# A hierarchical attention layer with a scan-like feed-forward part on one core: units of the feed-forward part in another order, last gate in halves, last norm on another engine

## The chip, the cores and the metric

The kernel runs on one core of a Trainium2 chip. The metric is device time in microseconds (us) of one execution; lower is better. A core has TensorE (PE, with its weight loads PEld), VectorE (DVE), ScalarE (ACT), GpSimd (POOL) and SyncE (SP), which here issues all DMAs. Each engine works through its own queue of instructions in order, and the queues meet at semaphores.

## The reference, cut to what matters

```python
# x: 2 x 2048 tokens of 256; attention with 16 heads and hierarchical levels
x = layernorm(x + attention(x))
# feed-forward: x is read as T = 2 steps of B = 2048 rows, 256 wide
c = broadcast(in_c)
for xt in x:                                    # two steps, t = 0 and 1
    f = sigmoid(xt @ wf.T + c @ uf.T + bf)
    i = sigmoid(xt @ wi.T + c @ ui.T + bi)
    g = tanh(xt @ wc.T + c @ uc.T + bc)
    c = f * c + i * g                           # c1 after t = 0, c2 after t = 1
h = tanh(x @ wo.T + c @ uo.T + bo)              # c2's product is shared by both t
out = layernorm(x + h)
```

In the first step c is the same for every row, so `c @ u.T` is one small product (`first_bias`); in the second step it is a full one.

## The kernel before

All of x (4096 tokens) stays in SBUF as `xs`, 32 tiles of 128 tokens. Attention runs in steps s = -3 to 140 over 32 chunks; the loop over `STEPS` in each engine's program sets what it issues in a step. The feed-forward part begins at step `FIRST_FFN` = 127 and lies at first beside the last steps of attention; the order of its units is written out by hand in `ffn_units` (L114), one unit per step, all the rest in the last step. Every engine walks the same list `UNITS` and does its own share of each unit.

The 2048 rows are four blocks `blk` of 512. Products are split in three for exactness (`mm3`, L370: high x high, high x low, low x high), so each product of 256 x 256 costs, for each half `mt` of 128 output features, two k x three matmuls of 128x512.

- `("t", blk, t)`, `turn_block` (L580 PE, L807 ACT, L1137 DVE): TensorE turns four tiles of `xs` into two banks (`turned`: banks 4 and 5), ScalarE copies the high half `yH`, VectorE subtracts for the low half `yL`.
- `("g", blk, t, mt)`, `gates` (L598, L815, L1143, L1326): three gates n = 0, 1, 2 into the three banks of `ring[mt]`; for t = 1, each gate is 6 matmuls with x and then 6 with c1. `GATE` numbers these units. ScalarE applies sigmoid or tanh into `gb`; VectorE forms the new c (three operations for c2, two for c1); ScalarE copies the high half (`c1H`, `c2H`), GpSimd (VectorE in the last block) subtracts for the low half (`c1L`, `c2L`). The first c1 product of a block waits for `g_c1l`.
- `("o", n)`, `outputs` (L625, L844, L1165, L1339): 128 rows of both t. TensorE forms the c2 product (`Ba`, bank 4) and then the two x products (`Bb`, bank 5), 18 matmuls of 128x256; from n = 12 on the banks are those of `ring`. VectorE adds the bias (`cu`) and both (`hh`); ScalarE applies tanh; GpSimd adds `hh` to `xs`. One unit later `out_stats` (L1179, VectorE) and `root` (L1317, GpSimd: variance + eps, then power -0.5); two units later `out_norm` (L1190, VectorE: two `tensor_scalar`, subtract the mean and multiply), and SyncE stores the 256 KB of tiles n and n + 16 when `d_out` allows.

All elementwise helpers stand at one line per engine: L365 and L368 are TensorE's matmul and transpose, L704 ScalarE's activation, L905 and L908 VectorE's two- and three-input operations, L1257 GpSimd's two-input operation, L1193 and L1197 the two normalisations. YB (bank 5) is also attention's bank for its last projection, whose result VectorE adds into `oo`; the turn of block 1 waits for it (`d_oo`).

Of the kernel before, what the change touches and what calls it, by code (L numbers as in the profile page):

```python
# [113 lines left out]
def ffn_units():  # L114
    units = [("t", 0, 0), ("t", 0, 1), ("g", 0, 0, 0), ("g", 0, 0, 1)]
# [12 lines left out]
GATE = {u[1:]: n for n, u in enumerate([u for u in UNITS if u[0] == "g"])}  # L128
TURN = {u[1:]: n for n, u in enumerate([u for u in UNITS if u[0] == "t"])}
YUSE = {u: n for n, u in enumerate([u for u in UNITS if u[0] == "t" or (u[0] == "o" and u[1] < 16)])}  # L130


def units_at(s):
    if s < FIRST_FFN:
        return []
    if s == FIRST_FFN:
        return UNITS[:2]
    n = s - FIRST_FFN + 1
    return UNITS[n:] if s == STEPS[-1] else UNITS[n:n + 1]


def program(nc, x, xT, wqk, wtok, wout, wffn, cst, bcv, fv, out):
    ctx = ExitStack()
    with ctx:  # L144
# [34 lines left out]
        lr3 = sb("lr3", [P, NC])  # L179

# [83 lines left out]
        a_c1, a_c2, a_hh = sem("a_c1"), sem("a_c2"), sem("a_hh")  # L264
# [24 lines left out]
        def _(e):  # L289
# [73 lines left out]
        def _(e):  # L363
# [234 lines left out]
            def gates(blk, t, mt):  # L598
                y, idx = blk % 2, GATE[blk, t, mt]
                for n in range(3):  # L600
                    if idx >= 2:
                        e.wait_ge(a_g, 3 * (idx - 2) + n + 1)
                    elif n == 0:
                        e.wait_ge(d_b0, 1)
                    if n == 0:
                        e.wait_ge(d_y[1], YUSE["t", blk, t] + 1)
                    if idx == 1 and n == 1:

                        e.wait_ge(d_y[1], 2)
                    if idx == 1 and n == 2:  # L610
                        e.wait_ge(m_free[1], len([m for m, u in MISC.values() if m == 1]))
                    for k in range(2):
                        c = wcol(WF + n, mt)
                        m = mm3(ring[mt][n][:, :], wH[:, k, c], wL[:, k, c], yH[t][y][:, k, :], yL[t][y][:, k, :],
                                k == 0, k == 1 and not t)
                    if t:
                        if n == 0:
                            e.wait_ge(g_c1l, 2 * blk + 2)
                        for k in range(2):
                            c = wcol(UF + n, mt)  # L620
                            m = mm3(ring[mt][n][:, :], wH[:, k, c], wL[:, k, c], c1H[y][:, k, :], c1L[y][:, k, :],
                                    False, k == 1)
                    m.then_inc(p_gate, 1)

            def outputs(n):  # L625
# [13 lines left out]
                for k in range(2):  # L639
# [19 lines left out]
            for s in STEPS:  # L659
# [32 lines left out]
                for u in units_at(s):  # L692
                    if u[0] == "g":
                        gates(*u[1:])
# [7 lines left out]
        def _(e):  # L702
# [112 lines left out]
            def gates(blk, t, mt):  # L815
                y, idx = blk % 2, GATE[blk, t, mt]
                for n in range(3):
                    e.wait_ge(p_gate, 3 * idx + n + 1)
                    if n == 0:
                        if idx == 0:  # L820
                            e.wait_ge(d_b0, 1)
                        if blk or t:

                            p = 2 * blk + mt - (0 if t else 2)
                            if t:
# [46 lines left out]
            for s in STEPS:  # L872
# [17 lines left out]
                for u in units_at(s):  # L890
# [4 lines left out]
                    elif u[1] < 16:  # L895
                        outputs(u[1])
# [572 lines left out]
```

## Time and profile before

| | |
|---|---|
| median of 3 runs | 742.78 us (740.77 to 743.75) |
| profiled execution | 742.03 us |
| its span | 739.9 us |
| PE busy | 690.9 us (93%) |
| DVE busy | 506.7 us (68%) |
| POOL busy | 356.7 us (48%) |
| ACT busy | 323.0 us (44%) |
| first matmul of the gates | 567.69 us |
| last matmul of the outputs starts | 726.61 us |
| last vector instruction starts | 736.96 us |

The span is what the profiler recorded of one execution; the 2.1 us beside it lie before the first and after the last record. "<-" in a row stands between what an instruction writes and what it reads, or names the instruction that released it. The timelines merge like instructions (x2 and so on). The feed-forward part is what comes after about 563 us.

### The profile page before, as it was taken

To read this page: it belongs to the slowest core of one execution; us is meant where nothing else is said; L and a number is where in the kernel's file an instruction comes from. 1 tells how busy PE (TensorE), PEld (TensorE's weight loads), DVE (VectorE), ACT (ScalarE), POOL (GpSimd) and SP (SyncE) were. 2 spreads that over 40 slices of the span, in tenths; PEclk is the share of its full clock that TensorE was granted. 3 is DMA by queue.
4 is the path that set the end of the run, shared out by engine and by line. 5 is a ranking of instruction groups with operands and counts; after the bars stand their busy time and mean duration, and the time that the engine had idled before them with its cause. 6 is when DMAs were issued, how large, how long until landed. Compare 5 with 4: busy or idle time off the path is not lost. (4 is left out here: it accounts for less than half of the span.)

```text
span 739.9 us, 21966 instructions
## 1 busy us (share of the span) xinstructions
PE 690.9 (93%) x9136; PEld 597.2 (81%) x9136; DVE 506.7 (68%) x1092; ACT 323.0 (44%) x708; POOL 356.7 (48%) x462
## 2 busy tenths in 40 slices
PE   6889999999999999999999999999979899999982
PEld 3778888888888888888888888888867678787872
DVE  2754776968787777757678776969774255575757
ACT  4545444453545443454555344453533233434321
POOL 1655564645556464646546554645462234252415
PEclk9999999999999999999999999999988999999997
DMA  8123030313225030203313040311230000010102
GB/s 283 29 48 84 9 90 14 80 25 67 47 47 91 3 91 3 62 23 70 63 31 90 3 91 9 83 31 49 49 102 2 0 1 15 14 44 16 43 14 86
DMA packets 53587, 37.08 MB, mean 50 GB/s; under 512 B 5360, under 2 KB 52080, under 8 KB 53488
## 3 DMA queue, kind: packets, MB, share of 16 engines
q1 hardware_dynamic: 53488, 35.67, 19.4%
q8 instruction: 73, 1.20, 0.7%
q14 instruction: 26, 0.21, 0.1%
HBM read 30.41 MB, written 5.24 MB: 48 GB/s over the span
## 5 line engine op out<-in xcount | busy, mean ns | idle before, releaser
L365 PE MATMUL bank<-xH,wH 128*128 128x256 f32 x480 | 145.5, 303 | 1.7 <-ACT KT L704 1.5
L365 PE MATMUL bank<-xL,wH 128*128 128x256 f32 x480 | 135.3, 282 | 0.0
L365 PE MATMUL bank<-xH,wL 128*128 128x256 f32 x480 | 135.2, 282 | 0.0
L905 DVE TENSOR_TENSOR W<-bank,E 128x512 f32<-128x512 f32 x128 | 82.1, 684 | 55.6 <-PE bank L365 55.0
L365 PEld LDWEIGHTS bank<-xH,wH 128*128 128x128 f32 x480 | 90.9, 189 | 14.0 <-issue 13.2
L365 PEld LDWEIGHTS bank<-xL,wH 128*128 128x128 f32 x480 | 91.2, 190 | 0.0
L365 PEld LDWEIGHTS bank<-xH,wL 128*128 128x128 f32 x480 | 90.9, 189 | 0.0
L704 ACT ACTIVATE QT<-bank 128x512 f32<-128x512 f32 x64 | 38.2, 597 | 106.0 <-PE bank L365 106.0
L365 PE MATMUL bank<-QT,KT 64*128 64x128 f32 x1024 | 74.4, 285 | 0.0
L704 ACT ACTIVATE E<-bank 128x512 f32<-128x512 f32 x128 | 66.1, 604 | 16.6 <-PE bank L387 16.6
L704 ACT ACTIVATE KT<-bank 128x512 f32<-128x512 f32 x64 | 38.3, 598 | 79.8 <-PE bank L365 79.7
L365 PEld LDWEIGHTS bank<-QT,KT 64*128 64x128 f32 x1024 | 62.1, 187 | 11.4 <-issue 5.1
L1257 POOL TENSOR_TENSOR lr<-mv,cs 128x1 f32<-128x1 f32 (+1 forms) x80 | 17.6, 220 | 92.2 <-DVE mv L1058 75.6
L905 DVE TENSOR_TENSOR g<-g 128x512 f32<-128x512 f32 x24 | 16.6, 692 | 63.3 <-ACT g L704 63.0
L1257 POOL TENSOR_TENSOR rs<-lr,cs 128x1 f32<-128x1 f32 (+1 forms) x80 | 56.2, 703 | 6.3
L1257 POOL TENSOR_TENSOR t<-t 128x416 f32<-128x416 f32 x45 | 48.6, 1081 | 3.6
L1257 POOL TENSOR_TENSOR xL<-xt,xH 128x512 fp32r<-128x512 f32 x15 | 19.3, 1289 | 63.8 <-ACT xH L704 63.8
L419 PE MATMUL bank<-W,V 128*32 128x128 f32 x1024 | 41.7, 281 | 2.9 <-DVE oo L905 2.9
L1257 POOL TENSOR_TENSOR x<-oo,xs 128x256 f32<-128x256 f32 x32 | 23.5, 735 | 40.2 <-DVE oo L908 40.2
L1257 POOL TENSOR_TENSOR prod<-ll,cs 128x512 f32<-128x512 f32 x32 | 41.3, 1291 | 0.5 <-DVE ll L905 0.5
L905 DVE TENSOR_TENSOR pre<-bank,bv 128x208 f32<-128x208 f32 x32 | 12.0, 374 | 42.8 <-PE bank L365 42.8
L704 ACT ACTIVATE t<-t 128x416 f32<-128x416 f32 x64 | 35.1, 549 | 10.6 <-DVE t L1088 6.7
(146 smaller groups left out, 1708.6 us busy)
## 6 DMA issues: line engine op xcount, KB each, us to landing
cB<-scr SPq DMA_DIRECT2D x240, 64.0 KB, 2.9
xt<-in_xT SPq DMA_DIRECT2D x16, 256.0 KB, 3.2
xs<-in_x SPq DMA_DIRECT2D x16, 256.0 KB, 4.1
out<-xs SPq DMA_DIRECT2D x16, 256.0 KB, 2.1
xt<-in_wffn SPq DMA_DIRECT2D x8, 256.0 KB, 2.9
QT<-in_wqk SPq DMA_DIRECT2D x4, 256.0 KB, 5.9
KT<-in_wqk SPq DMA_DIRECT2D x4, 256.0 KB, 6.3
scr<-cT SPq DMA_DIRECT2D x16, 64.0 KB, 1.9
```

Of the source, the lines that this page charges most:

```text
L365: return e.matmul(o, a, b, start=start, stop=stop)
L419: y = e.matmul(YB[32 * n:32 * n + 32, 128 * k:128 * k + 128], V[sg % 3][:, c, v:v + 32], W[:, h, :], start=u == 0 and k == 0, stop=u == 1, ...
L704: return e.activation(o, i, f, **kw)
L905: return e.tensor_tensor(o, a, b, op)
L1257: return e.tensor_tensor(o, a, b, op)
```

## The change

- The unit `g` is taken apart: `x` is one gate's products with x, `c` one gate's products with c1. A list of groups (`GROUPS`) takes the place of one unit per step. For t = 1 and mt = 0 the three x products come first and then the c products; for mt = 1 x and c alternate gate by gate. Turns of t = 1 stand between two gates of a unit.
- Output units are spread: each has gates between it and the next one. An output's x products now come ahead of its c2 product.
- The last gate unit (block 3, t = 1, mt = 1) is two units `h` of 256 rows each; gates, cells, copies and subtractions are done by halves. The last four outputs use other banks (`LAST`).
- The last layernorm: GpSimd forms mean x rstd (`nm3`) after the root; ScalarE negates it (`nb3`) and normalises with scale and bias; tile 31 alone stays with VectorE (`last_norm`). In outputs 13 and 15 VectorE adds `hh` to `xs` in place of GpSimd. The stores wait for `a_out`.

The diff, cut to its core:

```diff
+def ffn_groups():
+    def g0(blk, mt):
+        return [("x", blk, 0, mt, n) for n in range(3)]
+    def g1(blk):
+        return [u for n in range(3) for u in (("x", blk, 1, 1, n), ("c", blk, 1, n))]
+    out = [[("t", 0, 0), ("t", 0, 1)], g0(0, 0), g0(0, 1)]
     for blk in range(4):
-        def o(k):
-            return ("o", 4 * blk - 4 + k) if 4 * blk - 4 + k >= 0 and blk + k // 4 > 0 else None
+        x, c = [[(k, blk) + ((1,) if k == "x" else ()) + (0, n) for n in range(3)] for k in "xc"]
+        if blk == 0:
+            out += [x, c]
+        else:
+            out += [x[0:2] + [("o", 4 * blk - 2)] + x[2:3] + c[0:1] + [("o", 4 * blk - 1)] + c[1:3]]
         if blk < 3:
-            units += [u for u in (("g", blk, 1, 0), o(3), ("t", blk + 1, 0), ("g", blk, 1, 1),
-                                  ("t", blk + 1, 1), ("g", blk + 1, 0, 0), o(4), ("g", blk + 1, 0, 1), o(5), o(6)) if u]
-        else:
-            units += [("g", blk, 1, 0), ("g", blk, 1, 1), o(3)]
-    return units + [("o", n) for n in range(12, 18)]
-UNITS = ffn_units()
-GATE = {u[1:]: n for n, u in enumerate([u for u in UNITS if u[0] == "g"])}
+            g, a = g1(blk), g0(blk + 1, 1)
+            out += [[("t", blk + 1, 0)], g[0:4] + [("t", blk + 1, 1)] + g[4:6], g0(blk + 1, 0)]
+            out += [[("o", 4 * blk)] + a[0:2] + [("o", 4 * blk + 1)] + a[2:3]]
+    return out + [[("h", h, n) for h in range(2) for n in range(3)], [("o", n) for n in range(12, 18)]]
+GROUPS = ffn_groups()
+UNITS = [u for g in GROUPS for u in g]
 TURN = {u[1:]: n for n, u in enumerate([u for u in UNITS if u[0] == "t"])}
 YUSE = {u: n for n, u in enumerate([u for u in UNITS if u[0] == "t" or (u[0] == "o" and u[1] < 16)])}
+LAST = {12: (3, 6), 13: (4, 5), 14: (7, 0), 15: (1, 2)}
...
-                e.wait_ge(d_out, n + 1)
+                e.wait_ge(a_out, n + 1)
+                if n == 15:
+                    e.wait_ge(d_out, 1)
...
+            def gate_x(blk, t, mt, n):
+                y, idx = blk % 2, 4 * blk + 2 * t + mt
+                if idx >= 2:
+                    e.wait_ge(a_g, 3 * (idx - 2) + n + 1)
+                elif n == 0:
+                    e.wait_ge(d_b0, 1)
+                if n == 0:
+                    e.wait_ge(d_y[1], YUSE["t", blk, t] + 1)
+                if idx == 1 and n == 1:
+                    e.wait_ge(d_y[1], 2)
+                if idx == 1 and n == 2:
+                    e.wait_ge(m_free[1], len([m for m, u in MISC.values() if m == 1]))
+                for k in range(2):
+                    c = wcol(WF + n, mt)
+                    m = mm3(ring[mt][n][:, :], wH[:, k, c], wL[:, k, c], yH[t][y][:, k, :], yL[t][y][:, k, :],
+                            k == 0, k == 1 and not t)
+                if not t:
                     m.then_inc(p_gate, 1)
...
+            def gate_c(blk, mt, n):
+                y = blk % 2
+                if n == 0 and mt == 0:
+                    e.wait_ge(g_c1l, 2 * blk + 2)
+                for k in range(2):
+                    c = wcol(UF + n, mt)
+                    m = mm3(ring[mt][n][:, :], wH[:, k, c], wL[:, k, c], c1H[y][:, k, :], c1L[y][:, k, :],
+                            False, k == 1)
+                m.then_inc(p_gate, 1)
...
+            def gate_h(h, n):
+                r = slice(256 * h, 256 * h + 256)
+                e.wait_ge(a_g, 3 * (13 + h) + n + 1)
+                for k in range(2):
+                    c = wcol(WF + n, 1)
+                    mm3(ring[1 - h][n][:, 0:256], wH[:, k, c], wL[:, k, c], yH[1][1][:, k, r], yL[1][1][:, k, r],
+                        k == 0, False)
+                for k in range(2):
+                    c = wcol(UF + n, 1)
+                    m = mm3(ring[1 - h][n][:, 0:256], wH[:, k, c], wL[:, k, c], c1H[1][:, k, r], c1L[1][:, k, r],
+                            False, k == 1)
+                m.then_inc(p_gate, 1)
...
             def outputs(n):
                 blk, q = n // 4, n % 4
                 y, use = blk % 2, YUSE["o", n]
                 c = slice(128 * q, 128 * q + 128)
-                Ba, Bb = banks[4:6] if n < 12 else ring[n % 2][0:2]
-                if n < 12:
-                    e.wait_ge(d_y[0], use)
+                Ba, Bb = [banks[i] for i in LAST.get(n, (4, 5))]
+                if n in (12, 14, 15):
+                    e.wait_ge(a_g, 48 if n == 12 else 51)
                 else:
-                    e.wait_ge(a_g, 3 * len(GATE))
-                    e.wait_ge(d_y[1], use - 1)
-                if blk < 3:
-                    e.wait_ge(g_c2l, 2 * blk + 2)
-                else:
-                    e.wait_ge(d_c2l, 2)
-                for k in range(2):
-                    m = mm3(Ba[:, 0:256], c2H[y][:, k, c], c2L[y][:, k, c], wH[:, k, wcol(UO)], wL[:, k, wcol(UO)],
-                            k == 0, k == 1)
-                m.then_inc(p_o, 1)
-                if n < 12:
-                    e.wait_ge(d_y[1], use)
+                    e.wait_ge(d_y[1], use if n < 12 else use - 1)
                 for t in range(2):
                     for k in range(2):
                         m = mm3(Bb[:, 256 * t:256 * t + 256], yH[t][y][:, k, c], yL[t][y][:, k, c],
                                 wH[:, k, wcol(WO)], wL[:, k, wcol(WO)], k == 0, k == 1)
+                m.then_inc(p_o, 1)
+                if blk < 3:
+                    e.wait_ge(g_c2l, 2 * blk + 2)
+                else:
+                    e.wait_ge(d_c2l, 2 if n < 14 else 3)
+                for k in range(2):
+                    m = mm3(Ba[:, 0:256], c2H[y][:, k, c], c2L[y][:, k, c], wH[:, k, wcol(UO)], wL[:, k, wcol(UO)],
+                            k == 0, k == 1)
                 m.then_inc(p_o, 1)
...
+            def gate_h(h, n):
+                r = slice(256 * h, 256 * h + 256)
+                e.wait_ge(p_gate, 45 + 3 * h + n + 1)
+                if h == 0 and n == 0:
+                    e.wait_ge(d_c1, 8)
+                act(gb[1][n][:, r], ring[1 - h][n][:, 0:256], ACT.Tanh if n == 2 else ACT.Sigmoid,
+                    bias=fvs[:, 3 + n:4 + n]).then_inc(a_g, 1)
+                if n == 2:
+                    e.wait_ge(d_c2, 8 + h)
+                    act(c2H[1][:, 1, r], gb[1][1][:, r], ACT.Copy).then_inc(a_c2, 1)
             def outputs(n):
                 i = n % 2
                 e.wait_ge(d_y[1], YUSE["o", n] + 1)
                 act(hh[i][:, :], hh[i][:, :], ACT.Tanh).then_inc(a_hh, 1)
+            def out_norm(n):
+                e.wait_ge(g_rs3, n + 1)
+                act(nb3[:, n:n + 17:16], nm3[:, n:n + 17:16], ACT.Copy, scale=-1.0).then_inc(a_nb, 1)
+                e.wait_ge(a_nb, n + 1)
+                for c in (n, n + 16) if n < 15 else (n,):
+                    a = act(xs[:, c, :], xs[:, c, :], ACT.Identity, scale=rs3[:, c:c + 1], bias=nb3[:, c:c + 1])
+                a.then_inc(a_out, 1)
...
+            def cells_h(h):
+                nonlocal made
+                f, i, c = [g[:, 256 * h:256 * h + 256] for g in gb[1]]
+                r = slice(256 * h, 256 * h + 256)
+                e.wait_ge(a_g, 45 + 3 * h + 3)
+                tt(i, i, c, ALU.mult).then_inc(d_own, 1)
+                tt(f, f, c1[1][:, 1, r], ALU.mult).then_inc(d_own, 1)
+                made += 2
+                e.wait_ge(d_own, made)
+                tt(i, f, i, ALU.add).then_inc(d_c2, 1)
+                e.wait_ge(a_c2, 8 + h)
+                tt(c2L[1][:, 1, r], i, c2H[1][:, 1, r], ALU.subtract).then_inc(d_c2l, 1)
...
             def outputs(n):
                 i, use = n % 2, YUSE["o", n]
-                Ba, Bb = banks[4:6] if n < 12 else ring[n % 2][0:2]
-                e.wait_ge(p_o, 2 * n + 1)
+                Ba, Bb = [banks[i] for i in LAST.get(n, (4, 5))]
+                e.wait_ge(p_o, 2 * n + 2)
                 if n >= 2:
                     e.wait_ge(d_y[1], YUSE["o", n - 2] + 1)
                 tt(cu[i][:, :], Ba[:, 0:256], bv[:, B_BO:B_BO + 256], ALU.add).then_inc(d_y[0], 1)
                 h3 = hh[i][:, :].rearrange("p (t n) -> p t n", t=2)
-                e.wait_ge(p_o, 2 * n + 2)
                 e.wait_ge(d_y[0], use + 1)
-                if n >= 2:
+                if n >= 2 and n - 2 != 13:
                     e.wait_ge(g_hh, n - 1)
                 tt(h3, Bb[:, :].rearrange("p (t n) -> p t n", t=2), bc(cu[i][:, :], 1, 2), ALU.add).then_inc(d_y[1], 1)
             def out_stats(n):
                 nonlocal made
                 i = n % 2
-                e.wait_ge(g_hh, n + 1)
+                if n not in (13, 15):
+                    e.wait_ge(g_hh, min(n + 1, 14))
+                else:
+                    e.wait_ge(a_hh, n + 1)
+                    dst = xs[:, n:n + 17:16, :]
+                    tt(dst, dst, hh[i][:, :].rearrange("p (t n) -> p t n", t=2), ALU.add).then_inc(d_own, 1)
+                    made += 1
+                    e.wait_ge(d_own, made)
                 for t in range(2):
                     e.bn_stats(st3[:, 2 * i + t, :], xs[:, n + 16 * t, :]).then_inc(d_own, 1)
                     made += 1
...
                 for t in range(2):
                     e.bn_aggr(mv3[:, n + 16 * t, :], st3[:, 2 * i + t, :]).then_inc(d_mv3, 1)
-            def out_norm(n):
-                nonlocal made
-                e.wait_ge(g_rs3, n + 1)
-                e.tensor_scalar(xs[:, n, :], xs[:, n, :], mv3[:, n, 0:1], rs3[:, n:n + 1], ALU.subtract,
-                                ALU.mult).then_inc(d_own, 1)
-                made += 1
-                n += 16
-                e.tensor_scalar(xs[:, n, :], xs[:, n, :], mv3[:, n, 0:1], rs3[:, n:n + 1], ALU.subtract,
+            def last_norm():
+                e.wait_ge(g_rs3, 16)
+                e.tensor_scalar(xs[:, 31, :], xs[:, 31, :], mv3[:, 31, 0:1], rs3[:, 31:32], ALU.subtract,
                                 ALU.mult).then_inc(d_out, 1)
...
-                            root(rs3[:, n:n + 17:16], lr3[:, n:n + 17:16], mv3[:, n:n + 17:16, 1], g_rs3)
+                            r = slice(n, n + 17, 16)
+                            root(rs3[:, r], lr3[:, r], mv3[:, r, 1], g_own)
+                            made += 1
+                            e.wait_ge(g_own, made)
+                            tt(nm3[:, r], mv3[:, r, 0], rs3[:, r], ALU.mult).then_inc(g_rs3, 1)
```

## Rows read from the trace of the kernel before

**Rows 1.** Busy time by stretch: PE, PEld, DVE, ACT, POOL, PE clock, DMA.

```profile
620.00:660.00 40.00, 38.26 (x207) 32.07 (x206) 24.43 (x50) 15.39 (x26) 14.66 (x18) 1.00 0.08 27
```

**Rows 2.** Waits of TensorE, 562 to 740 us: total, times, longest.

```profile
PE bank L365 <- POOL c1L L1257: 2.9, 1, 2.9
PE bank L368 <- DVE cu L905: 2.3, 2, 1.2
...
PE bank L368 <- DVE oo L905: 2.0, 1, 2.0
PE bank L365 <- DVE cu L905: 1.6, 3, 0.5
```

**Rows 3.** Timeline of TensorE: start, us, what, idle time before it and releaser.

```profile
581.41 0.50 PE L365 MATMUL bank<-c1H,wH 128*128 128x512 f32 x1 [2.89 <-POOL c1L L1257]
...
582.91 0.61 PE L365 MATMUL bank<-yH,wH 128*128 128x512 f32 x1
...
586.31 0.41 PE L365 MATMUL bank<-c1H,wL 128*128 128x512 f32 x1
...
616.67 0.39 PE L365 MATMUL bank<-wH,c2H 128*128 128x256 f32 x1 [0.52 <-DVE cu L905]
...
630.79 1.34 PE L368 MATMUL bank<-cs,xs 128*128 128x128 f32 x8 [1.16 <-DVE cu L905]
```

**Rows 4.** Busy time in a stretch of 2 us, columns as in rows 1.

```profile
584.00:586.00 2.00, 2.00 (x6) 1.51 (x6) 0.00 (x0) 0.00 (x0) 0.00 (x0) 0.50 0.00 0
```

**Rows 5.** Timeline of TensorE, end of the last gate and output 11.

```profile
711.28 0.40 PE L365 MATMUL bank<-c1L,wH 128*128 128x512 f32 x1
711.51 0.40 PE L365 MATMUL bank<-c1H,wL 128*128 128x512 f32 x1
...
713.61 0.28 PE L365 MATMUL bank<-wL,yH 128*128 128x256 f32 x1
713.73 0.28 PE L365 MATMUL bank<-wH,yL 128*128 128x256 f32 x1
```

**Rows 6.** Timeline of VectorE in the tail: one period, and the last row.

```profile
715.99 0.42 DVE L905 TENSOR_TENSOR cu<-bank,bv 128x256 f32<-128x256 f32 x1
716.50 0.69 DVE L905 TENSOR_TENSOR hh<-bank,cu 128x512 f32<-128x512 f32 x1
717.11 0.74 DVE L1184 BATCH_NORM_STATS2 st<-xs 128x6 f32<-128x256 f32 x2
...
718.05 1.31 DVE L1193 TENSOR_SCALAR xs<-xs,mv,rs 128x256 f32<-128x256 f32 x1
...
719.61 0.41 DVE L905 TENSOR_TENSOR cu<-bank,bv 128x256 f32<-128x256 f32 x1
...
736.96 0.41 DVE L1197 TENSOR_SCALAR xs<-xs,mv,rs 128x256 f32<-128x256 f32 x1
```

**Rows 7.** Timeline of GpSimd: one root among attention's end, and one period.

```profile
609.50 1.07 POOL L1257 TENSOR_TENSOR rs<-lr,cs 128x1 f32<-128x1 f32 x1
...
717.93 1.28 POOL L1257 TENSOR_TENSOR xs<-xs,hh 128x512 f32<-128x512 f32 x1 [17.72 <-ACT hh L704]
719.17 0.24 POOL L1257 TENSOR_TENSOR lr<-mv,cs 128x2 f32<-128x2 f32 x1
719.49 0.75 POOL L1257 TENSOR_TENSOR rs<-lr,cs 128x2 f32<-128x2 f32 x1
```

**Rows 8.** Groups of ScalarE: count, busy us, mean ns, idle before.

```profile
L704 ACT ACTIVATE g<-bank,fvs 128x512 f32<-128x512 f32 x24 | 16.5, 687 | 45.7 <-PE bank L365 45.4
...
L704 ACT ACTIVATE V<-bank 128x128 f32<-128x128 f32 x64 | 14.3, 275 | 33.6 <-DVE pre L905 33.6
L704 ACT ACTIVATE hh<-hh 128x512 f32<-128x512 f32 x16 | 10.1, 632 | 26.1 <-DVE hh L905 26.1
...
L704 ACT ACTIVATE yH<-bank 128x512 fp32r<-128x512 f32 x16 | 8.9, 588 | 9.4 <-PE bank L368 9.4
...
L704 ACT ACT_TABLE_LOAD x1 | 1.3, 1283 | 0.0
```

More of the change, by code:

```diff
@@ L179, in program @@
         lr3 = sb("lr3", [P, NC])
+        nm3 = sb("nm3", [P, NC])
+        nb3 = sb("nb3", [P, NC])
         first = ExitStack()
@@ L596, in turn_block @@
                     y.then_inc(p_turn, 1)
[L598 to L611, printed above, removed]
-                    for k in range(2):
[L613 to L622, printed above, removed]
-                    m.then_inc(p_gate, 1)
@@ L692, in _ @@
                 for u in units_at(s):
-                    if u[0] == "g":
-                        gates(*u[1:])
+                    if u[0] == "x":
+                        gate_x(*u[1:])
+                    elif u[0] == "c":
+                        gate_c(*u[1:])
+                    elif u[0] == "h":
+                        gate_h(*u[1:])
                     elif u[0] == "t":
@@ L813, in turn_block, with gate @@
                     act(yH[t][i][:, k, :], turned(blk, k)[:, :], ACT.Copy).then_inc(a_yh, 1)
[L815 to L825, printed above, removed]
-                                e.wait_ge(d_c1, 2 * blk + mt + 1)
-                            else:
-                                e.wait_ge(d_c2, p + 1)
-                                e.wait_ge(a_c2, p + 1)
-                                e.wait_ge(g_c2l, p + 1)
-                    bias = fvs[:, 3 * mt + n:3 * mt + n + 1] if t else b0[:, mt, n:n + 1]
-                    act(gb[mt][n][:, :], ring[mt][n][:, :], ACT.Tanh if n == 2 else ACT.Sigmoid, bias=bias).then_inc(a_g, 1)
+            def gate(blk, t, mt, n):
+                y, idx = blk % 2, 4 * blk + 2 * t + mt
+                e.wait_ge(p_gate, 3 * idx + n + 1)
+                if n == 0:
+                    if idx == 0:
+                        e.wait_ge(d_b0, 1)
+                    if blk or t:
+                        p = 2 * blk + mt - (0 if t else 2)
+                        if t:
+                            e.wait_ge(d_c1, 2 * blk + mt + 1)
+                        else:
+                            e.wait_ge(d_c2, p + 1)
+                            e.wait_ge(a_c2, p + 1)
+                            e.wait_ge(g_c2l, p + 1)
+                bias = fvs[:, 3 * mt + n:3 * mt + n + 1] if t else b0[:, mt, n:n + 1]
+                act(gb[mt][n][:, :], ring[mt][n][:, :], ACT.Tanh if n == 2 else ACT.Sigmoid, bias=bias).then_inc(a_g, 1)
+                if n < 2:
+                    return
                 if t == 0:
@@ L890, in _ @@
                 for u in units_at(s):
-                    if u[0] == "g":
-                        gates(*u[1:])
+                    if u[0] == "x" and u[2] == 0:
+                        gate(*u[1:])
+                    elif u[0] == "c":
+                        gate(u[1], 1, *u[2:])
+                    elif u[0] == "h":
+                        gate_h(*u[1:])
                     elif u[0] == "t":
                         turn_block(*u[1:])
-                    elif u[1] < 16:
-                        outputs(u[1])
+                    elif u[0] == "o":
+                        if u[1] < 16:
+                            outputs(u[1])
+                        if 0 <= u[1] - 2 < 16:
+                            out_norm(u[1] - 2)
         @block.vector
@@ L1226, in _ @@
                 for u in units_at(s):
-                    if u[0] == "g":
-                        gates(*u[1:])
+                    if u[0] == "x" and u[2] == 0 and u[4] == 2:
+                        cells(*u[1:4])
+                    elif u[0] == "c" and u[3] == 2:
+                        cells(u[1], 1, u[2])
+                    elif u[0] == "h" and u[2] == 2:
+                        cells_h(u[1])
                     elif u[0] == "t":
                         turn_block(*u[1:])
-                    else:
+                    elif u[0] == "o":
                         if u[1] < 16:
@@ L1362, in _ @@
                 for u in units_at(s):
-                    if u[0] == "g":
-                        gates(*u[1:])
+                    if u[0] == "x" and u[2] == 0 and u[4] == 2:
+                        gates(*u[1:4])
+                    elif u[0] == "c" and u[3] == 2:
+                        gates(u[1], 1, u[2])
                     elif u[0] == "o":
-                        if u[1] < 16:
+                        if u[1] < 16 and u[1] not in (13, 15):
                             outputs(u[1])
```

26 lines of the change are left out of this document (10 added, 16 removed).

## The prediction

> **What bounds the kernel now.** I read the busy table by stretches first [rows 1]: TensorE works 38.3 of 40 us in the feed-forward part, ScalarE 15.4. So that part is bound by TensorE until its matmuls end, and a tail by something else. Next come the waits of TensorE after 562 us [rows 2]: 2.9 us for `c1L` (GpSimd's low half of c1), 2.0 for `oo` (the vector add that frees bank 5 of attention's last projection), 2.3 and 1.6 for `cu` (the vector add behind which banks 4 and 5 come free). The timeline shows where they stand [rows 3]: 2.89 us before the first c1 product, then in each block 0.52 us between two output units and 1.16 us before a turn; three of the first and two of the second, 3.88 us in all, which are the 2.3 and 1.6 of [rows 2]. The 2.89 are followed by a stretch whose granted clock is 0.50, the lower level of 1.2 GHz [rows 4].
>
> The last gate's matmuls end at 711.51 + 0.23 = 711.74 us [rows 5], and the last vector instruction at 736.96 + 0.41 = 737.37 [rows 6]. The tail belongs to VectorE. Its period in [rows 6], from the `cu` at 715.99 to the next: cu 0.51, hh 0.61, two statistics and two aggregates 0.94, then both normalisations 1.56 until 719.61: 3.6 us, and 1.31 of it is the first normalisation. That first normalisation is the telling row: the same shape takes 0.41 in the last row. It starts 0.12 us after GpSimd's add of 1.28 us [rows 7] and ends 0.15 us after that add's end. The Trainium skill, SBUF — State Buffer, on the shared port pair, says that a VectorE operation in a two-port mode and a GpSimd operation block each other for a whole instruction; by that rule, the trace agrees, and the cost goes away when the normalisation leaves VectorE.
>
> The profiled execution took 742.03 us for a span of 739.9, so 2.13 lie around the span; the median of the runs is 742.78, 0.75 above it. I sum against 742.03 and add 0.75 at the end.
>
> **x products ahead of c1's.** No matmul is added. Ahead of the first c1 product, TensorE now has the x products of all three gates instead of one: 2 x 6 matmuls at 0.233 us [rows 5], 2.8 us of cover. The stall was 2.89, and attention's last projection (four matmuls) now also falls ahead of the c1 products: stall gone, -2.9. The stretch at half clock after it [rows 4] held eight matmuls from 582.91 to 586.31 us [rows 3], 3.4 us where 8 x 0.233 = 1.9: without the idle time before it, -1.5. I take both, since the stretch starts right behind the stall; that the clock dips all the same is in the range.
>
> **Turns and projection.** The projection of the last chunk stood right ahead of the turn that needs its bank, which cost the 2.0 us of `oo` [rows 2]. Now 18 matmuls (4.2 us) lie between, far more than an add of 0.42: -2.0.
>
> **Outputs apart.** In the steady blocks, between two users of banks 4 and 5 there is now gate work of at least 2.8 us. cu and hh want 0.51 + 0.69 = 1.2 us [rows 6]. The five stalls [rows 3] go: -3.9. What is late next? (a) ScalarE, in order: after an output's tanh (0.63) it now runs the sign copy and two normalisations, then the two waiting gates. Priced below, that puts the gates' end at 4.5 us after the output's matmuls, cells (0.69 x 3) at 6.6, the c2 copy at 7.2, the turned block's copies and subtractions at 9.1. TensorE wants that bank for the next turn at 9.4 (gates 2.8, a turn of about 1.0, where [rows 3] has 1.34 behind a stall, gates 5.6): 0.3 us to spare. (b) In the group o, x, x, o, x, counted from the first output's end, the second's hh is there at 6.1 us, tanh 6.7, norms 8.1, the last x gate 8.8, cells 10.2, copy 10.8, GpSimd's subtraction (1.3, as its add in [rows 7]) 12.1; TensorE wants it at 12.6 (six gate parts of 1.4 us, two outputs of 2.1): 0.5 to spare. So I take no stall, but the cover is thin.
>
> **Last gate in halves of rows.** Twelve matmuls of 512 columns become 24 of 256, 0.233 against 0.117 us [rows 5]: nothing on TensorE. The first half's cells end while the second half's matmuls run. Before, `cu` followed T0 (end of the last gate) by 715.99 - 711.74 = 4.25 us. Four VectorE steps shrink by 0.28 (0.69 to 0.41, [rows 6]), two on ScalarE by 0.2 each (512 columns 0.59, 128 columns 0.28 [rows 8], so about 0.38 for 256): 2.6 us. TensorE doesn't wait, for outputs 12 and 13 and the x part of 14 cover 5.6 us.
>
> **Output 11** moves ahead of T0: 18 matmuls at 0.117, +2.1.
>
> So T0 = 711.74 + 2.1 - 2.9 - 1.5 - 2.0 - 3.9 = 703.5.
>
> **The last norm on ScalarE, the sign and one product.** No row shows this activation with a scale and a bias from memory. A gate with a bias pointer takes 0.69, the plain copy of the same bank 0.59 [rows 8], so a pointer is 0.10. For 256 columns: 0.38 + 0.04 (from SBUF, 0.63 against 0.59) + 0.20 = 0.61, the second about 0.5 behind the first. Bounds: 0.38 without price for pointers, 0.69, a whole gate. The sign copy is between 0.2 and 0.28 [rows 8] (its 128-column row); I take 0.25 with its own wait. So 1.4 us per output on ScalarE, 2.0 with the tanh. In a sentence of its own: by the Trainium skill, ScalarE: Activation LUTs, "What ACT_TABLE_LOAD costs", an activation is 186 ns + 0.833 ns per column + 93 per pointer, which would be 0.585; the sum hardly moves. On GpSimd a product of two columns is added per output, 0.25 as `lr` [rows 7]: root and product 1.35. In outputs 13 and 15 VectorE does the add (0.69) in place of GpSimd (1.28).
>
> **The tail, from T0**, each engine in order. VectorE: cu, hh of 12 at 2.6 to 3.7, statistics 11 to 4.7, hh 13 to 5.8, statistics 12 to 6.7, hh 14 to 7.9, add and statistics 13 to 9.5, hh 15 to 10.6, statistics 14 to 11.5. ScalarE: norm 11 waits for GpSimd's root 11 (7.2), so tanh 14 ends at 9.2, norm 12 at 10.6, tanh 15 at 11.2. VectorE: add and statistics 15 to 13.1. GpSimd: add 14 to 10.5, root 13 to 11.9, root 14 to 13.2, root 15 to 14.6. Last norm on ScalarE: sign, wait, 0.61: 15.5. VectorE's last norm, 0.41, ends before it. Behind a two-input vector operation a one-column root took 1.07 us, where even a two-column one takes 0.75 [rows 7]; the adds 13 and 15 can do that once each: +0.3. The tail is 15.8 us. Before, from the same point (713.8, behind output 11) it was 737.37 - 713.8 = 23.5.
>
> The last instruction ends at 703.5 + 15.8 = 719.3; before, 2.5 us of output transfer followed; span 721.8, execution 723.9, on the median's level 724.7. I say **725**.
>
> **Rivals.** (1) The cover is thin, chance 0.25. ScalarE waits in order for GpSimd's root and for VectorE's hh; each is behind others. If (a) and (b) come 0.7 us too late in each of three blocks (+4) and the tail loses the port twice more (+2), the time is about 731. For it: GpSimd and VectorE hold each other up already [rows 6, 7]. Against: ScalarE is busy 15 of 40 us [rows 1], and the norms add 1.1 x 4 per block. (2) The clock dips as before, 0.10: +1.5, 726.5. (3) Slower, 0.04: a table switch. ScalarE loads a table for 1.28 us [rows 8]. If this activation were not in the set of sigmoid and tanh, each output would cost two loads, 2.6 us. Then (a) comes 2.3 and (b) 2.1 us too late, 13 us in three blocks, and the tail goes at 4.6 us an output on ScalarE, +9; 725 + 22 = 747. It decides as soon as a load stands between tanh and norm. Against: the copies between sigmoids needed no load, one load stands in the whole feed-forward part. By the Trainium skill, ScalarE: Activation LUTs, on table sets, identity is in every set; no row here shows this function, and it would leave 725. (4) Only one side pays, 0.05: if new waits take back all of TensorE's 10.3 us, 742.8 - 23.5 + 15.8 = 735; if the tail keeps its 23.5, 733. The forecast itself has 0.56.
>
> **Range.** Low end: the norm at 0.38 and no port loss, 721. High end: it takes in rival 1 whole, 731. Outside are rivals 3 and 4 and a part of each end. A measurement of this kernel can tell about 0.5%, 3.7 us. All cases but 3 and a worse form of 4 are over that: faster 0.92, same 0.04, slower 0.04.
>
> **What would show it.** No wait of TensorE over 0.5 us between 578 us and the tail, above all none before the first c1 product; the granted clock whole from about 567 us on to the last outputs; the last gate's end near 703.5; no normalisation of 1.3 us on VectorE; ScalarE's norm about 0.6 and no second table load; 15 to 16 us from the last gate to the last norm. Waits of ScalarE's sign copy for GpSimd ahead of gates that TensorE then waits for would make it rival 1; table loads, rival 3.

## The result, and the profile after

The changed kernel takes 720.09 us (median of 4 runs, 717.82 to 721.02) where the kernel before takes 743.26 beside it: ratio 0.9685, 95% interval 0.9654 to 0.9716, faster. I had said 725, range 721 to 731. The direction and the mechanisms held; the gain is 23 us where my sum had 18, and the time lies 0.9 us below the range. The same code ran twice more beside other experiments, at 720.33 and at 723.52 us. The page of the profiled execution (721.02 us):

```profile
span 719.2 us, 22059 instructions
...
PE 683.2 (95%) x9172; PEld 595.7 (83%) x9172; DVE 486.0 (68%) x1067; ACT 340.2 (47%) x759; POOL 356.6 (50%) x476
...
PEclk9999999999999999999999999999999899999998
```

TensorE's waits after 562 us (total, times, longest) are one row, which was there before too, at the very start of the part. All four waits of [rows 2] are gone, and so is one of 2.2 us for `c2L` in the tail of before:

```profile
PE bank L381 <- DVE yL L964: 0.7, 1, 0.7
```

Where [rows 3] had 2.89 us of idle time ahead of the first c1 product, TensorE now goes from x products to attention's last projection and on (timeline: start, us, what):

```profile
581.49 1.02 PE L378 MATMUL bank<-wo,yt 128*128 128x256 f32 x4
582.16 0.58 PE L378 MATMUL bank<-c1H,wH 128*128 128x512 f32 x1
```

The last gate ends at 701.15 us. VectorE's tail, as in [rows 6]: cu, hh and statistics follow each other in 2.0 us for the first output (2.2 for the next, 2.7 where VectorE also adds), no normalisation between them, and one at the very end.

```profile
703.89 0.42 DVE L964 TENSOR_TENSOR cu<-bank,bv 128x256 f32<-128x256 f32 x1
704.34 0.69 DVE L964 TENSOR_TENSOR hh<-bank,cu 128x512 f32<-128x512 f32 x1
704.95 0.74 DVE L1262 BATCH_NORM_STATS2 st<-xs 128x6 f32<-128x256 f32 x2
...
705.90 0.39 DVE L964 TENSOR_TENSOR cu<-bank,bv 128x256 f32<-128x256 f32 x1
...
714.22 0.25 DVE L1266 BATCH_NORM_AGGREGATE mv<-st 128x2 f32<-128x6 f32 x2
715.81 0.41 DVE L1270 TENSOR_SCALAR xs<-xs,mv,rs 128x256 f32<-128x256 f32 x1 [1.34 <-POOL nm L1334]
```

ScalarE's norm, in the tail (705.61, 705.83) and for output 15: the sign copy 0.19 to 0.21 us, one normalisation 0.60, two 1.09.

```profile
705.61 0.19 ACT L736 ACTIVATE nb<-nm 128x2 f32<-128x2 f32 x1
705.83 1.09 ACT L736 ACTIVATE xs<-xs,nb,rs 128x256 f32<-128x256 f32 x2
...
715.81 0.21 ACT L736 ACTIVATE nb<-nm 128x2 f32<-128x2 f32 x1
716.05 0.60 ACT L736 ACTIVATE xs<-xs,nb,rs 128x256 f32<-128x256 f32 x1
```

Three stretches tell more than the total. The head is all before the first gate's first matmul, which the change doesn't touch. The gate stretch goes from there to the end of the last gate. The tail goes on to the end of the last normalisation; the last store adds 2.5 us in both kernels.

| kernel | median, us | ratio to before, 95% interval | head | gate stretch | tail |
|---|---|---|---|---|---|
| before | 743.26 | 1 | 567.69 | 144.05 | 25.63 |
| changed | 720.09 | 0.9685 (0.9654 to 0.9716) | 568.01 | 133.14 | 15.50 |
| e1_together | 727.32 | 0.9811 (0.9755 to 0.9867) | 564.78 | 141.86 | 15.50 |
| e2_xfirst | 737.88 | 0.9968 (0.9932 to 1.0004) | 567.03 | 140.36 | 25.59 |
| e3_norm_act | 736.86 | 0.9932 (0.9906 to 0.9959) | 566.22 | 144.38 | 21.01 |
| e4_norm_dve | 723.60 | 0.9760 (0.9696 to 0.9824) | 564.61 | 133.14 | 18.77 |
| e5_whole | 724.64 | 0.9762 (0.9713 to 0.9811) | 567.60 | 133.01 | 21.04 |
| e6_pool_adds | 721.52 | 0.9728 (0.9655 to 0.9800) | 564.55 | 133.14 | 16.54 |
| e8_forced | 737.41 | 0.9925 (0.9895 to 0.9955) | 565.50 | 151.04 | 15.51 |
| e9_again | 723.52 | 0.9730 (0.9666 to 0.9793) | 571.70 | 133.14 | 15.51 |
| e12_control | 720.33 | 0.9696 (0.9651 to 0.9741) | 565.02 | 133.14 | 15.51 |
| e10_bias24 | 716.62 | 0.9655 (0.9616 to 0.9694) | 563.29 | 133.13 | 15.53 |
| e11_bias_split | 721.45 | 0.9696 (0.9657 to 0.9734) | 563.80 | 133.14 | 15.52 |

The medians and ratios come from the timed runs, the three stretches from one profile each. Each ratio is taken to the kernel before as it ran beside that kernel, at 743.26 us for the changed kernel, 740.88 for e1 to e4, 742.30 for e5 to e9 and 742.21 for e10 to e12, so ratios can be compared between groups and medians can't. The changed kernel ran three times (e9_again and e12_control are the same code): gate stretch and tail agree to 0.01 us, while the head moves by 6.7 us. So the stretches are what the experiments are read by.

### The profile page after: what moved, and what is told of

The parts are those of the page before. It is cut to its first block, busy times and chain, and to the rows that moved or that the text cites. A ratio compares the mean times of both kernels' runs of the same rounds, so it can differ in the third digit from the quotient of the medians.

```text
span 719.2 us, 22059 instructions
## 1 busy us (share of the span) xinstructions
PE 683.2 (95%) x9172; PEld 595.7 (83%) x9172; DVE 486.0 (68%) x1067; ACT 340.2 (47%) x759; POOL 356.6 (50%) x476
## 4 chain that ended last, share of the span: by engine, by line
PE 83%; DVE 10%; issue 3%; ACT 2%; POOL 2%; DMA 1%; SPq 0%; DVEq 0%
PE bank L378 61%; PE bank L381 6%; PE bank L400 4%; PE bank L467 4%; PE bank L432 4%; PE bank L496 3%; DVE W L964 2%; DVE S L964 1%; DVE zt L964 1%; DVE t L967 1%; DMA bv<-in_bcv 1%; ACT t L736 0%; POOL t L1334 0%; ACT E L736 0%; DVE C L1184 0%
## 5 line engine op out<-in xcount | busy, mean ns | idle before, releaser
L964 DVE TENSOR_TENSOR g<-g 128x512 f32<-128x512 f32 (+1 forms) x26 | 17.6, 676 | 35.0 <-ACT g L736 34.7
L400 PE MATMUL bank<-CT,AT 32*128 32x128 f32 x1024 | 38.5, 288 | 2.0 <-DVE CT L1189 2.0
```

The lines of the kernel that those rows point to most:

```text
L400: m = e.matmul(XP[q][:, :].rearrange("p (h t) -> p h t", h=H)[:, :, 8 * j:8 * j + 8], AT[b][r, j, :], CT[b][r, :].rearrange("p (h t) -> p ...
L964: return e.tensor_tensor(o, a, b, op)
```

## The experiments

The prediction's sum for the gate stretch was 144.05 + 2.1 - 2.9 - 1.5 - 2.0 - 3.9 = 135.85 us. Measured: 133.14. So 2.7 us of the 4.6 that I missed lie there (the tail and the time around the span give 0.3 each, the head takes 0.3 back, and the rest is the step to the median). Theory R, the prediction's: a stall costs what its idle row says. Theory S: it costs more, from the last matmul's start to the time at which the flow is regular again. The rival: the outputs' stalls have no part in it. The rows of the kernel before already speak for S, when starts are compared instead of idle times (TensorE, first between two outputs, then at a turn):

```profile
615.87 0.28 PE L365 MATMUL bank<-wH,yL 128*128 128x256 f32 x1
616.67 0.39 PE L365 MATMUL bank<-wH,c2H 128*128 128x256 f32 x1 [0.52 <-DVE cu L905]
616.89 0.28 PE L365 MATMUL bank<-wL,c2H 128*128 128x256 f32 x1
...
630.79 1.34 PE L368 MATMUL bank<-cs,xs 128*128 128x128 f32 x8 [1.16 <-DVE cu L905]
631.89 0.48 PE L365 MATMUL bank<-yH,wH 128*128 128x512 f32 x1
```

The row of 615.87 is a matmul of 256 columns, regularly followed by the next after 0.117 us. It was followed after 0.80: 0.68 lost, and the row says 0.52, since a matmul's record (0.28 us) is longer than the spacing. The first matmul after the stall takes 0.22 to the next start instead of 0.117: 0.10 more. At the turn the eight transposes and what follows them take 1.10 us where an unstalled turn takes 0.79: 0.31 more.

**One kind of stall, eleven times.**

```diff
                 m.then_inc(p_o, 1)
+                if n < 11:
+                    e.wait_ge(d_y[1], use + 1)
```

> The changed kernel with a wait added to TensorE: behind each of outputs 0 to 10 it waits until VectorE has written that output's hh, so eleven stalls of one known kind stand in the steady blocks. Theory R (a stall costs its idle row): the stretch from the first gate to the end of the last one grows by the sum of the idle rows, about 11 x 1.2 = 13 us. Theory S (a stall costs from start to start): it grows by about 0.3 us more for each, 16 to 17 us. If the clock falls behind idle times of this length, it grows by more than that; the kernel before had none behind its stalls of 1.2 us.

The idle rows sum to 14.4 us (waits of TensorE):

```profile
PE bank L378 <- DVE hh L966: 14.4, 11, 1.5
```

The gate stretch grew by 17.9 us. In this run it began at half clock, which cost its first three matmuls 0.6 (0.60, 0.43 and 0.38 us from start to start instead of 0.34, 0.23 and 0.23). The other 17.3 are 2.9 more than the idle rows, 0.26 us for each stall. One of them, from start to start:

```profile
607.61 0.28 PE L378 MATMUL bank<-wH,c2L 128*128 128x256 f32 x1
609.13 0.50 PE L378 MATMUL bank<-yH,wH 128*128 128x512 f32 x1 [1.24 <-DVE hh L966]
609.47 0.40 PE L378 MATMUL bank<-yL,wH 128*128 128x512 f32 x1
```

1.52 us where 0.117 is regular, then 0.34 where 0.233 is: 1.51 lost for a row of 1.24. Theory S holds. The granted clock stayed whole behind all eleven.

**The outputs back together.**

```diff
-            out += [x[0:2] + [("o", 4 * blk - 2)] + x[2:3] + c[0:1] + [("o", 4 * blk - 1)] + c[1:3]]
+            out += [[("o", 4 * blk - 2)] + x + c + [("o", 4 * blk - 1)]]
...
-            out += [[("o", 4 * blk)] + a[0:2] + [("o", 4 * blk + 1)] + a[2:3]]
+            out += [[("o", 4 * blk)] + a + [("o", 4 * blk + 1)]]
```

> The changed kernel with the output units put back next to each other, as they stood before (outputs 1 and 2, 5 and 6, 9 and 10 in pairs; 3 and 7 right before a turn); all else as changed. Theory R (a stall costs its idle row, as the prediction summed it): five stalls, 3.9 us, so the last gate ends about 705.0 us and the time is 724. Theory S (a stall costs from start to start, with the refill behind it and the slower first matmuls): 0.87 x 3 + 1.71 x 2 = 6.0 us, time 726. Theory N (the two us that the prediction missed have nothing to do with the outputs' place): 3.9 or less, and the excess over the nominal spacing stays below 0.2 us beside the idle rows.

```profile
PE bank L378 <- DVE hh L964: 4.0, 3, 1.4
PE bank L381 <- DVE cu L964: 2.3, 2, 1.2
```

The stretch grew by 8.7 us, 0.8 of them again a start at half clock. So 7.9 for idle rows of 6.3: 1.6 more for five stalls, 0.32 each. The rows themselves are not those of before: with its x products first, an output waits in bank 5 for the previous output's hh (1.25 to 1.4 us), where before it waited in bank 4 for cu (0.52). So both sizes that I had expected, 3.9 and 6.0, were too low, but their order stands: the cost exceeds the rows. The place of the outputs sets it.

**The x products first, alone.** In the kernel before, TensorE's loop over the three gates of a unit (t = 1, mt = 0) forms all x products and only then the c1 products.

```diff
...
+                    if t and mt == 0 and n < 2:
+                        continue
+                    for n in range(3) if t and mt == 0 else [n] if t else []:
...
```

> The kernel before with one change: for t = 1 and mt = 0 TensorE issues the x products of all three gates ahead of the first c1 product. If the clock's dip follows from the idle time ahead of it, stall and dip go together: 3.1 + 1.6 = -4.7 us, 738.5. If the dip comes anyway: -3.1, 740. If the wait only moves (c1L comes as late and the 2.8 us do not cover it, or the turn's stall grows): above 741.

The gate stretch is 3.7 us shorter, 4.3 without the 0.6 that its start at half clock cost (first row: busy times, then the granted clock). Where [rows 4] has 0.50, the clock is now whole:

```profile
566.00:568.00 2.00, 2.00 (x19) 1.42 (x19) 1.60 (x3) 1.86 (x2) 0.00 (x0) 0.50 0.03 8
...
582.00:584.00 2.00, 2.00 (x10) 1.64 (x9) 0.00 (x0) 0.69 (x1) 0.12 (x1) 1.00 0.00 0
584.00:586.00 2.00, 2.00 (x10) 1.61 (x10) 0.00 (x0) 0.79 (x2) 0.00 (x0) 1.00 0.00 0
```

The dip followed the idle time: stall and dip went together. The 4.3 compare with 2.9 + 1.5 in the sum. They are not all that the stall and the dip cost: without the projection ahead of it, the first c1 product still came 0.52 us behind the last x product where 0.233 is regular (580.88 to 581.40 us), and its first gap was 0.10 longer. With these the two cost 4.7, as Theory S has it (3.2 + 1.5). The ratio's interval includes 1, so the median proves nothing here; the reading rests on the stretch of one profile.

**The norm on ScalarE, alone.** The kernel before with the changed kernel's sign copy, normalisations and product.

```diff
+            def out_norm(n):
+                e.wait_ge(g_rs3, n + 1)
+                act(nb3[:, n:n + 17:16], nm3[:, n:n + 17:16], ACT.Copy, scale=-1.0).then_inc(a_nb, 1)
...
```

> The kernel before with one change: the last norm of all 16 outputs on ScalarE (sign copy, scale and bias), the product on GpSimd. Stalls of TensorE stay. Tail: VectorE's period falls from 3.6 to 2.1 us, and GpSimd becomes the bound at 1.3 + 1.35 = 2.65 us per output: 5 x 1.0 = -5 us, 738. If the norm's removal gives the whole 1.5 us per output: -7.5, 735.5. If ScalarE's waits for GpSimd hold up the gates in the steady blocks: above 740.

The tail fell by 4.6 us and the gate stretch grew by 0.3. GpSimd is the bound, as expected: it works without a pause at 2.4 us per output, and VectorE waits for its add (1.38 us, last row).

```profile
726.57 1.26 POOL L1268 TENSOR_TENSOR xs<-xs,hh 128x512 f32<-128x512 f32 x1
727.79 0.19 POOL L1268 TENSOR_TENSOR lr<-mv,cs 128x2 f32<-128x2 f32 x1
728.06 0.70 POOL L1268 TENSOR_TENSOR rs<-lr,cs 128x2 f32<-128x2 f32 x1
728.83 0.20 POOL L1268 TENSOR_TENSOR nm<-mv,rs 128x2 f32<-128x2 f32 x1
```

```profile
727.86 0.75 DVE L1197 BATCH_NORM_STATS2 st<-xs 128x6 f32<-128x256 f32 x2 [1.38 <-POOL xs L1268]
```

**The norm back on VectorE.**

```diff
-                        if u[1] == 17:
-                            last_norm()
+                        if 0 <= u[1] - 2 < 16:
+                            out_norm(u[1] - 2)
...
```

> The changed kernel with the last norm back on VectorE (two operations per output, no sign copy, no product on GpSimd); outputs apart, halves and x first stay. Tail: five norms of 1.56 us come back on VectorE, less what GpSimd bound: +5 to +7 us, 725 to 727. In the steady blocks nothing if the new places cover VectorE's 1.56 us more per output; stalls before the turns otherwise, +1 per block.

Gate stretch the same to 0.01 us: the new places of the outputs cover VectorE's norms as well. Tail +3.3 us, less than the 5 to 7. The reason stands in VectorE's rows: of the first norms of six outputs only the one that starts right behind the start of GpSimd's add takes 1.32 us. One more, at 709.40 us, meets the last 0.4 us of an add and takes 0.57. The others take 0.38 to 0.41, since with the adds of 13 and 15 on VectorE there are fewer to meet.

```profile
702.50 1.32 DVE L1267 TENSOR_SCALAR xs<-xs,mv,rs 128x256 f32<-128x256 f32 x1
...
706.06 0.38 DVE L1267 TENSOR_SCALAR xs<-xs,mv,rs 128x256 f32<-128x256 f32 x1
...
712.21 0.38 DVE L1267 TENSOR_SCALAR xs<-xs,mv,rs 128x256 f32<-128x256 f32 x1
```

By the rule of the Trainium skill on the shared port pair (SBUF — State Buffer, "Who interferes with whom"), the trace agrees: the same operation costs 0.38 or 1.32 us by what GpSimd does at that moment.

**The last gate whole.** One unit of 512 rows; output 12 starts in banks that are free.

```diff
-    return out + [[("h", h, n) for h in range(2) for n in range(3)], [("o", n) for n in range(12, 18)]]
+    return out + [g1(3), [("o", n) for n in range(12, 18)]]
...
-LAST = {12: (3, 6), 13: (4, 5), 14: (7, 0), 15: (1, 2)}
+LAST = {12: (0, 1), 13: (4, 5), 14: (2, 3), 15: (6, 7)}
...
```

> The changed kernel with the last gate unit whole (512 rows, as before) and the banks of the last four outputs chosen so that output 12 can start at once; all else as changed. The prediction's term: the first cu comes 4.25 us behind the last gate where the halves give 2.75: +1.5 us in the tail, by VectorE. Rival: TensorE stalls for c2L behind output 12's x part (about 3 us idle), its clock falls, outputs 13 to 15 come late and the tail grows by 3 us or more.

The tail grew by 5.5 us, so the rival won. TensorE waits for c2L and its granted clock falls to 0.50; VectorE, which no longer has the norms to do, waits for TensorE twice:

```profile
705.00 0.58 PE L378 MATMUL bank<-wH,c2H 128*128 128x256 f32 x1 [2.81 <-DVE c2L L964]
```

```profile
706.00:708.00 2.00, 2.00 (x12) 2.00 (x11) 1.28 (x3) 0.13 (x1) 0.00 (x0) 0.50 0.00 0
```

```profile
706.68 0.42 DVE L964 TENSOR_TENSOR cu<-bank,bv 128x256 f32<-128x256 f32 x1 [1.74 <-PE bank L378]
...
710.52 0.42 DVE L964 TENSOR_TENSOR cu<-bank,bv 128x256 f32<-128x256 f32 x1 [1.75 <-PE bank L378]
```

How much of the 5.5 us is the stall and how much the clock, this run doesn't separate. The kernel before had such a stall too, with the clock at 0.51 from 716 to 718 us behind it:

```profile
PE bank L365 <- DVE c2L L905: 2.2, 1, 2.2
```

There VectorE needed 3.6 us per output, and none of its rows in the tail has a wait for TensorE of over 0.1 us. My term for the halves, 4.25 to 2.6 us, was the part on VectorE. The sum stood all the same, because I had worked out the new tail as a whole.

**The adds of 13 and 15 on GpSimd.**

```diff
-                        if u[1] < 16 and u[1] not in (13, 15):
+                        if u[1] < 16:
...
```

> The changed kernel with the adds of outputs 13 and 15 back on GpSimd. GpSimd's add takes 1.28 us where VectorE's takes 0.68, and output 15's add is on the last chain: +0.6 to +1 us in the tail if the chain through VectorE is bound by its work, 0 to +0.3 if VectorE's freed 1.3 us makes up for it, and more than +1.5 if GpSimd (root and product of 12 to 14) is busy when the add could start.

Tail +1.03 us, the upper end of the first case. VectorE now waits for GpSimd's add before each of the last three statistics (0.38 us for the first of them):

```profile
708.54 0.75 DVE L1255 BATCH_NORM_STATS2 st<-xs 128x6 f32<-128x256 f32 x2 [0.35 <-POOL xs L1327]
...
710.97 0.75 DVE L1255 BATCH_NORM_STATS2 st<-xs 128x6 f32<-128x256 f32 x2 [1.39 <-POOL xs L1327]
```

**The same code again, and the head.**

> The changed kernel once more, beside the three above. From the first gate to the end: 151.2 us as in its first profile, within 0.3. The place of the first gate (568.0 us then, 567.7 before, 564.6 to 567 in the other runs) lies ahead of everything that was changed: if it moves by 2 us or more between runs of the same kernel, the part of the miss that is not in the feed-forward part is that.

> The changed kernel without any edit, on the same chip as the two above. From its first gate to the end 151.2 us, as in both profiles of it; in the place of the first gate anything between 564 and 572 us.

Gate stretch plus tail plus store: 151.20 and 151.18 us, as in the first profile. The first gate stood at 571.70 and at 565.02. In e9_again the granted clock was at half from about 556 to 569.5 us:

```profile
558.00:562.00 4.00, 4.00 (x21) 4.00 (x20) 1.88 (x5) 0.00 (x0) 3.20 (x4) 0.50 0.00 0
...
566.00:570.00 4.00, 3.35 (x14) 2.60 (x13) 1.98 (x6) 1.19 (x2) 0.74 (x2) 0.56 0.00 0
```

In there lie the 36 matmuls of two columns of `first_bias`, at 0.21 us each from 557.67 us on. In the kernel before they start at 556.19 us with 0.11 us each, and the clock falls at 559.0, while they run and TensorE is busy by its records:

```profile
558.89 0.25 PE L365 MATMUL bank<-c0H,wH 128*128 128x2 f32 x1
559.00 0.35 PE L365 MATMUL bank<-c0L,wH 128*128 128x2 f32 x1
559.22 0.35 PE L365 MATMUL bank<-c0H,wL 128*128 128x2 f32 x1
```

**Fewer of these matmuls.** c0's high and low half are the two columns of one operand; 24 matmuls in place of 36, and VectorE adds the columns.

```diff
-                            t = mm3(banks[0][:, o:o + 2], wH[:, k, c], wL[:, k, c], c0H[:, k, :], c0L[:, k, :],
-                                    k == 0, k == 1)
+                            mm(banks[0][:, o:o + 2], wH[:, k, c], c0H[:, k, :], k == 0, False)
+                            t = mm(banks[0][:, o:o + 2], wL[:, k, c], c0H[:, k, :], False, k == 1)
...
```

> The changed kernel with one more change, ahead of the feed-forward part: first_bias forms c0's products with 24 matmuls of two columns in place of 36 (the two columns are the high and the low half of c0, VectorE adds them). In the profiles so far the 36 stand at 556 to 561 us, from 0.11 us each at the full clock to 0.21 at half clock, and the granted clock falls while they run and stays down until the first gates. If only their number counts: -1.3 to -2.5 us. If the clock also falls later or not at all: -3 to -5 us. Nothing if the vector engine's adds behind it set the first gate.

716.62 us against 720.33 for the changed kernel beside it (e12_control), 3.7 us less and the best median of all. The intervals of the two ratios overlap, so this is likely and not shown. In its profile the clock stays whole through the small matmuls:

```profile
554.00:558.00 4.00, 4.00 (x54) 3.67 (x53) 3.71 (x8) 0.63 (x1) 0.63 (x2) 1.00 0.10 32
558.00:562.00 4.00, 2.74 (x21) 2.38 (x20) 3.14 (x9) 1.09 (x2) 3.33 (x5) 1.00 0.00 0
562.00:566.00 4.00, 4.00 (x35) 3.02 (x34) 1.68 (x4) 3.10 (x4) 0.00 (x0) 1.00 0.00 0
```

**Half of them between the turns.**

```diff
                 if s == FIRST_FFN - 1:
-                    first_bias()
+                    first_bias(0)
...
                         turn_block(*u[1:])
+                        if u[1:] == (0, 0):
+                            first_bias(1)
...
```

> As the one before, and the second half of these matmuls (12) stands between the two turns of block 0, where TensorE waits 0.65 us for VectorE. If the clock falls because of the long row of small matmuls, the half clock ahead of the first gates goes: 2 us less than the one before. If it is VectorE's add of the bias that then comes late, the first gate waits: up to 1 us more.

Its profiled execution took 716.84 us with the clock whole, but its median is 721.45, no better than the changed kernel and not the 2 us less than e10_bias24 that I had expected.

In windows of 4 us, all 11 profiles with the 36 matmuls in one go (before, the changed kernel three times, seven experiments) have a granted clock of 0.69 or less somewhere from 554 to 566 us: 0.63 and 0.52 in before, 0.61 and 0.54 in the first profile of the changed kernel. The profiles of e10_bias24 and e11_bias_split have 1.00 throughout, and the two earliest gate starts of the table (563.29 and 563.80 against 564.55 to 571.70).

That the 36 matmuls are the cause is likely and not shown, for three reasons. The mean granted clock, which is known for every single run, speaks against a tie to them alone: where the profile shows no dip there, it is 0.988, and this stands at four of six runs of e10_bias24 (716.09 to 716.90 us), at one of six of e11_bias_split, and at one of six of e12_control, which has all 36 and took 716.96 us. All other runs of these three have 0.979 to 0.986 and took 718.03 to 724.67. In the 11 profiles the fall doesn't stand at one place either: in five it comes while the 36 run, in five up to 1.2 us after the last has started, and in e9_again 1.8 us ahead of the first, where TensorE had been idle for 1.93 us shortly before. And each of the two experiments has only one profile. What else spreads the heads (564.55 to 571.70, with the dip in all of them) stays open.

## Why the prediction was right and where it was wrong

The mechanisms were right. The step that failed is the pricing of TensorE's stalls: I put each at its idle row, 2.9 + 2.0 + 3.9 = 8.8 us, where from start to start they cost about 10.9, and the 3.9 for the outputs and turns alone were 5.6. The second one is the 0.75 us that I added to come from an execution to the median; there the changed kernel's median lay 0.93 us below its profiled execution. Of the 4.6 us between my 724.7 and the measured 720.09, 2.9 lie between the sum and its own execution (723.9 against 721.02), and 1.7 in the step from there to the median.

- **x ahead, turn and projection, outputs apart**: right in mechanism, each wait gone, and none came in their place. Mis-sized is one kind of term, the stalls. From start to start the first one cost 3.2 (581.41 - 578.12 less 0.23, and 0.1 for the first matmul), a pair of outputs 0.78 instead of 0.52, a turn 1.62 instead of 1.16. With the one at `oo` (2.1 instead of 2.0) that is over 2 us for the seven stalls, of the 2.7 that the gate stretch fell short of my sum. e8_forced shows the same excess on a stall of one kind. The remaining half microsecond I can't assign.
- **The clock's dip**: -1.5 was right: the eight matmuls from 582.91 us took 1.5 more than at the whole clock, and in e2_xfirst, which takes away nearly all of the idle time and nothing else, the dip is gone. I had taken it from the order of the rows alone.
- **Halves**: right in the sum for a reason that I had only half seen. The halves do not only shorten VectorE's chain by 1.6 us; they keep TensorE from a stall and a dip that would now be on the path (5.5 us in e5_whole).
- **Norm on ScalarE**: I said 0.61 us for one and 1.1 for two; measured 0.60 and 1.09. The sign copy took 0.19 to 0.21 (0.25 with its wait). By the formula of the Trainium skill (ScalarE: Activation LUTs, "What ACT_TABLE_LOAD costs"), an estimate is 0.585 for one: the trace agrees within 0.02. No second table load, so rival 3 falls.
- **Tail**: 15.8 forecast, 15.50 measured. GpSimd's small operations were held twice by VectorE's adds (0.55 to 0.56 instead of 0.20 us), as I had allowed for.
- **Cover**: I gave 0.25 to rival 1. TensorE waited nowhere. e4_norm_dve shows that the cover also holds with the norms on VectorE. It takes them off ScalarE at the same time, so it doesn't measure the room on ScalarE's chain, my 0.3 and 0.5 us; how large that was stays open.
- **The level**: I added 0.75 us because the median of before lay that much above its profiled execution. The changed kernel's median lies 0.93 below its own. The heads of the same code differ by 6.7 us, so one profiled execution says little on the side of the median on which the next kernel's will fall. The 0.9 us by which the median fell below the range are less than that: e9_again, the same code, took 723.52 us and lies within it. So where the median fell against the range's low end was in part chance. Here the range was too narrow: it had bounds for the norm and the port, but none for the head, nor for the price of a stall above its row. With 1 us for each, its low end would have been 719.

## What to carry to other kernels

Price a stall of TensorE from start to start, or by comparing a block that has it with one that hasn't: here 0.26 to 0.5 us on top of the idle row, for each. When an engine in a tail is relieved, look for the stalls that its slowness had covered: the halves were worth 1.6 us by the trace of before, and the tail was 5.5 us longer without them once VectorE was fast. And divide a long kernel at a fixed instruction: total times moved by several microseconds where the stretches repeated to 0.01.

## What the runs showed of the hardware

- TensorE's clock can fall to 1.2 GHz while its records are busy without a gap: in the kernel before at 559.0 us, between matmuls of two columns that took 0.11 us each ahead of it and 0.21 behind it. All 11 profiles with the 36 in one go have a dip beside them, which begins at most 1.8 us ahead of their first and 1.2 us behind the start of their last; the profiles of the two with 24, or with half of the 24 elsewhere, have none there. Whether the 36 cause it is open.
- Eleven idle times of 1.24 to 1.5 us, with 5 to 19 us of work between them, brought no dip (e8_forced); nor did the one of 2.0 for `oo` (before, e2_xfirst, e3_norm_act). Those of 2.81 (e5_whole) and 2.89 (before, e3_norm_act) did. One of 2.21 for `c2L` had half clock behind it in before and e2_xfirst and the whole clock in e3_norm_act (1.00 from 706 to 720 us, the wait ending at 715.08), so the length of an idle time alone doesn't decide.
- A VectorE operation with two inputs in SBUF holds up GpSimd's two-column operations, from 0.20 to 0.55 us (709.27 and 712.90 us in the changed kernel's profile). GpSimd's add of 512 columns holds a VectorE normalisation for as long as it lasts (0.38 to 1.32 us, e4_norm_dve).
